# Six of sixteen images: the last two slots' statistics taken one slot at a time, with the instruction streams merged anew

## What is computed

```python
x = x + conv_block(group_norm(x, groups=32))
# conv_block: 1x1 convolution 768 -> 16, four "experts" of a 3x3 convolution at
# four resolutions, weighed by a gate (top 2 of 4), 1x1 convolution 16 -> 768
h = mean(xc over pixels) @ H_w.T + H_b        # xc: the 16-channel images
g = softmax(h where among the top two, else -inf)
out = sum(experts * reshape(g, (4, 16, 1, 1, 1)))
```

## Time and profile before

| | |
|---|---|
| median of 3 runs | 1462.71 us (1459.87 to 1462.95) |
| the profiled execution's own time | 1463.79 us |
| its span, first to last instruction | 1462.1 us |
| busy: PE 1206.2, DVE 1028.5, ACT 661.6, POOL 314.9 us | 82%, 70%, 45%, 22% of the span |
| moved by the DMA engines | 540.01 MB, mean 369 GB/s |
| mean granted TensorE clock | 0.88 of full speed |

### The profile page before, as it was taken

One profiled execution on the slowest core, in us unless ns is written; L12 is line 12 of the kernel. 1 busy time (PEld: TensorE's weight loads), 2 busy tenths in 40 slices (PEclk: granted clock), 3 DMA queues, 4 the chain that ended last, 5 costly groups with the idle time before them and its releaser, 6 DMA issues.

```text
span 1462.1 us, 24056 instructions
## 1 busy us (share of the span) xinstructions
PE 1206.2 (82%) x8700; PEld 818.7 (56%) x8700; DVE 1028.5 (70%) x2747; ACT 661.6 (45%) x1549; POOL 314.9 (22%) x381
## 2 busy tenths in 40 slices
...
DMA  9798996699999999999999999999999999999998
GB/s 343 263 363 301 344 345 260 241 368 343 410 391 394 404 356 368 378 386 385 376 396 386 380 378 346 382 359 391 378 379 382 405 413 411 408 411 413 396 383 356
DMA packets 188162, 540.01 MB, mean 369 GB/s; under 512 B 12810, under 2 KB 12810, under 8 KB 188044
## 3 DMA queue, kind: packets, MB, share of 16 engines
...
## 4 chain that ended last, share of the span: by engine, by line
PE 43%; DMA 28%; DVE 13%; ACT 6%; SPq 5%; issue 4%; POOL 1%; DVEq 0%; ACTq 0%; POOLq 0%
PE ring_ps L680 15%; DMA x_sb<-in_x 14%; DMA out<-x_sb 14%; PE conv_ps L750 10%; DVE x_sb L1004 9%; PE ring_ps L781 8%; PE img_ps L697 8%; SPq L512 3%; ACT xT L803 3%; DVE stats L920 2%; SPq L483 1%; PE ring_ps L769 1%; ACT unread_copy L827 1%; ACT unread_squares L825 1%; PE ring_ps L710 1%
## 5 line engine op out<-in xcount | busy, mean ns | idle before, releaser
L1004 DVE TENSOR_TENSOR x_sb<-x_sb,ring_ps 128x768 f32<-128x768 f32 x512 | 460.4, 948 | 312.0 <-PE ring_ps L781 186.3
L920 DVE BATCH_NORM_STATS2 stats<-x_sb 128x6 f32<-128x192 f32 x1792 | 473.0, 343 | 44.7 <-DMA x_sb<-in_x 39.4
L803 ACT COPY xT<-ring_ps 128x1024 f32<-128x1024 f32 x384 | 376.3, 1012 | 228.9 <-PE ring_ps L680 165.4
L680 PE MATMUL ring_ps<-ident,x_sb 128*128 128x128 f32 x3072 | 399.8, 283 | 66.8 <-DMA x_sb<-in_x 25.4
L680 PEld LDWEIGHTS ring_ps<-ident,x_sb 128*128 128x128 f32 x3072 | 348.7, 145 | 146.4 <-issue 89.4
L781 PE MATMUL ring_ps<-w,es 128*128 128x512 f32 (+1 forms) x1024 | 334.5, 443 | 111.7 <-DVE x_sb L1004 84.4
L781 PEld LDWEIGHTS ring_ps<-w,es 128*128 128x128 f32 x1024 | 188.5, 229 | 237.9 <-DVE x_sb L1004 148.6
L643 POOL TENSOR_TENSOR band<-taps,masks 128x640 f32<-128x640 f32 (+1 forms) x112 | 133.0, 1204 | 492.9 <-PE conv_ps L750 489.1
L750 PE MATMUL conv_ps<-xc,band 128*128 128x1 f32 (+8 forms) x1120 | 235.1, 360 | 4.0 <-issue 2.7
L697 PE MATMUL img_ps<-xT,w 128*32 128x256 f32 x3072 | 218.4, 393 | 16.9 <-ACT xT L803 13.2
L750 PEld LDWEIGHTS conv_ps<-xc,band 128*128 128x128 f32 x1120 | 168.0, 207 | 79.0 <-issue 76.2
...
## 6 DMA issues: line engine op xcount, KB each, us to landing
x_sb<-in_x SPq DMA_DIRECT2D x128, 1536.0 KB, 11.4
out<-x_sb SPq DMA_DIRECT2D x256, 768.0 KB, 10.4
...
wl_raw<-in_L_conv_convl_w SPq DMA_DIRECT2D x8, 9.0 KB
gate_w<-in_L_conv_H_w SPq DMA_DIRECT2D x8, 0.2 KB
...
b_raw<-in_L_conv_conv_b SPq DMA_DIRECT2D x2, 3.0 KB
```

The costliest lines, as they stand in the source:

```text
L680: last = nc.tensor.transpose(ring_ps[:, buf, q, half * P:(half + 1) * P], slot("L", a, 2 * c + half)[:, q, k * P:(k + 1) * P], ident[:, :])
L803: nc.scalar.copy(xT[:, at % XT], ring_ps[:, TURN["T", a, n] % RING]).then_inc(xT_copied, 1)
L920: ins = nc.vector.bn_stats(stats[:, c, g, :], group)
L1004: nc.vector.tensor_tensor(x_sb[:, n, 2 * half + q % 2, :], x_sb[:, n, 2 * half + q % 2, :], flat_ps[:, TURN["E", b, t] % RING, 0:D], ALU.a ...
```

## The change

`SINGLE` was 0 and becomes 6: for the first six images of order A the last pair of slots (6 and 7) is no longer one part of the statistics but two, each of one slot. Their moments have five parts where there were four. An instruction over one slot has 96 elements per partition where one over two slots has 192. The instruction gives the same kind of moments for its halves, of half as many elements, so the means are halved first (a new DVE instruction on 128 x 56) and then squared. All four lists are merged anew; the pieces in them are the same but for the new ones (`B12.4`, `S12.4` and so on, the fifth parts). The number of transfers and their bytes are unchanged, and so are the places and `KEPT`.

```diff
-SINGLE = 0
+SINGLE = 6
...
 PE_ORDER
-... T12.17-18 ... T12.20-22 M12.18 T12.23 M12.19-20 Z0 M12.21 T0.0 ...
+... T12.17 ... T12.21-22 M12.20 T12.23 T0.0 Z0 M12.21 T0.1 ...
 ACT_ORDER
-S0.1.30-31 T12.7-12 S0.2.28-29 T12.13-15 S0.2.30-31 T12.16 S0.3.28 T12.17-19 S0.3.29 T12.20 S0.3.30-31 T12.21-23 S4.0.28 D0
+S0.1.30-31 T12.6-8 S0.2.28-30 T12.9 S0.2.31 T12.10-14 S0.3.28-29 T12.15 S0.3.30 T12.16-18 S0.3.31 T12.19 S0.4.28-29 T12.20 S0.4.30-31 T12.21-23 T0.0 D0
```

More of the change, by code:

```diff
@@ new lines @@
+S8.7.0 R14.3.1:7.1 S8.7.1 R14.4.0:0.0 S14.0.0 S14.0.1 S14.1.0 S14.1.1 S14.2.0 R14.4.1:0.1 R14.5.0:5.0 S14.2.1
+R14.5.1:5.1 R14.6.0:6.0 S14.3.0 S14.3.1 S14.4.0 S14.4.1 R14.6.1:6.1 R14.7.0:7.0 R14.7.1:1.0 R13.0.0:1.1 R13.0.1:7.1
+S14.5.0 S14.5.1 S14.6.0 R13.1.0:0.0 S14.6.1 S14.7.0 R13.1.1:0.1 R13.2.0:5.0 R13.2.1:5.1 R13.3.0:6.0 S14.7.1
+R13.3.1:6.1 S13.0.0 S13.0.1 S13.1.0 S13.1.1 S13.2.0 R13.4.0:7.0 R13.4.1:7.1 R13.5.0:1.0 R13.5.1:1.1 S13.2.1
+R13.6.0:0.0 R13.6.1:0.1 R13.7.0:5.0 R13.7.1:5.1 S13.3.0 S13.3.1 S13.4.0 S13.4.1 S13.5.0 S13.5.1 S13.6.0 S13.6.1
@@ L96 @@
+S13.7.0 S13.7.1 S15.0.0 S15.0.1 S15.1.0 S15.1.1 S15.2.0 S15.2.1 S15.3.0 R12.0.0:10.0 R12.0.1:6.0 R12.1.0:6.1 S15.3.1
+S15.4.0 S15.4.1 S15.5.0 S15.5.1 S15.6.0 R12.1.1:10.1 S15.6.1 S15.7.0 R12.2.0:9.0 R12.2.1:9.1 S15.7.1 S12.0.0
+R12.3.0:8.0 S12.0.1 R12.3.1:8.1 R12.4.0:10.0 S12.1.0 S12.1.1 S12.2.0 S12.2.1 R12.4.1:6.0 R12.5.0:7.0 R12.5.1:7.1
+S12.3.0 R12.6.0:6.1 R12.6.1:10.1 S12.3.1 S12.4.0 S12.4.1 R12.7.0:8.0 R12.7.1:8.1 S12.5.0 S12.5.1 S12.6.0 S12.6.1
+S12.7.0 S12.7.1
 """
 PE_ORDER = """
-V T12.0-3 Z12 T12.4 M12.0-4 T12.5-8 M12.5 T12.9-10 M12.6-8 T12.11-12 M12.9-10 T12.13 M12.11-12 T12.14-17 M12.13-14
@@ L143 @@
-M15.18-20 T15.21 X8.2 T15.22 E8.14 M15.21 T15.23 M15.22-23 E8.15 X8.3 G3 E8.16 H3 E8.17-30 C14.0-1 E8.31 C14.2-6
-X14.0-1 E14.0-9 C13.0 E14.10-13 C13.1 X14.2 E14.14-15 X14.3 E14.16-18 C13.2 E14.19 C13.3-6 E14.20-26 C15.0-5 E14.27-31
-X13.0-1 E13.0-13 C15.6 X13.2 E13.14-15 X13.3 E13.16-22 C12.0-1 E13.23 C12.2-4 E13.24-31 X15.0-1 E15.0-12 C12.5-6
-E15.13 X15.2 E15.14-15 X15.3 E15.16-31 X12.0-1 E12.0-13 X12.2 E12.14-15 X12.3 E12.16-31
+V T12.0-2 Z12 T12.3-5 M12.0-3 T12.6-8 M12.4-8 T12.9-12 M12.9-10 T12.13-14 M12.11 T12.15-16 M12.12 T12.17 M12.13-15
@@ new lines @@
+T12.18 M12.16-17 T12.19-20 M12.18-19 T12.21-22 M12.20 T12.23 T0.0 Z0 M12.21 T0.1 M12.22-23 T0.2 W T0.3 M0.0-1 T0.4
+M0.2 T0.5-7 M0.3-6 T0.8-9 M0.7-8 T0.10-12 M0.9-12 T0.13-17 M0.13-14 T0.18 M0.15 T0.19 M0.16 T0.20 M0.17 T0.21 M0.18-20
+T0.22 Z4 T0.23 M0.21 T4.0 M0.22 T4.1 M0.23 T4.2-3 M4.0 T4.4 M4.1 T4.5-6 M4.2-4 T4.7-9 M4.5-6 T4.10 M4.7 T4.11 M4.8
+T4.12 M4.9-10 T4.13-14 M4.11-12 T4.15-16 M4.13-14 T4.17 M4.15 T4.18 M4.16 T4.19 M4.17 T4.20 M4.18-19 T4.21-22 Z8 T4.23
+M4.20 T8.0 M4.21 T8.1 M4.22-23 T8.2 M8.0 T8.3 M8.1 T8.4-6 M8.2-3 T8.7 M8.4 T8.8 M8.5-6 T8.9 M8.7 T8.10 M8.8-9 T8.11
@@ L147 @@
+C12.4-6 E15.9-13 X15.2 E15.14-15 X15.3 E15.16-31 X12.0-1 E12.0-13 X12.2 E12.14-15 X12.3 E12.16-31
 """
 ACT_ORDER = """
[L152 to L155 removed]
@@ L171 @@
[L171 to L175 removed]
+S12.0.28-31 S12.1.28-31 S12.2.28-31 S12.3.28-30 T12.0 S12.3.31 S12.4.28-31 T12.1-2 D12 S0.0.28-31 S0.1.28 T12.3
```

229 lines of the change are left out of this document (111 added, 118 removed).

## The result

The changed kernel takes 1494.2 us (median of 4, 1485.6 to 1497.7), the kernel before in the same measurement 1462.8; the ratio is 1.0193, interval 1.015 to 1.0235. Timed again later beside experiments it took 1490.2 us (6 runs) for 1465.7: 1.0152, interval 1.012 to 1.0185. By the two ratios it is 22 to 28 us slower (by the medians 24 to 31). The direction was forecast; the size, 13 us with 1486 as the upper end, was about half.

What follows compares the result with a forecast made beforehand. DVE and ACT bound the early images, transfers the rest. 6.4 at image 0 plus four times 2.8 less 0.6 is 17.0; less 4.0 given back, 13.0 us: 1476 us, with 8 in 10 at 1462 to 1486.

Steps and rivals of the forecast that it cites:

- What bounds it: Early, DVE and ACT have nearly no room; late, transfers never stop, so a delay ahead of them moves the end.
- The price of slot by slot: First six images: finer statistics cost DVE 2.8 us an image (0.9 to 8.0) and ACT 2.0 us.
- Image 0: Four ACT copies move behind the load wait and groups take longer: fold +6.4 us, near 104.3, image 12's 2.8 included.
- Images 4, 8 and 3: DVE goes on back to back: each adds 2.8 us, less 0.6 once because image 4 no longer waits for W's transposition.
- Image 2: DVE back to back adds another 2.8 us; the fold ends at 277.7 for 260.8, 17.0 later in all.
- That last step: From Z2 to the first addition: 15.4 us for 19.4, as 6.85 us of convolution moves ahead of Z2; 4.0 given back.
- The late lists: New instruction lists after 300 us: not costed, taken as hidden under the transfers if they keep them fed.
- My own sign of being wrong: After 300 us: the forecast would be wrong if the transfer rate there, 381 GB/s, moved by more than 1%.
- the late transfers: Rival, 300 to 1200 us: better-mixed reads and writes give the delay back; faster, say 1457, chance 0.08; about all, 0.10.
- Price by elements: Rival on the statistics: 0.130 us a step, DVE 0.9 an image, ACT's 2.0 sets the pace; 1466 to 1469, chance 0.12.
- finer statistics: Rival at images 12 and 0: DVE starts sooner on single slots, at most 2.3 us each; 1459, chance 0.03.
- ACT and PE jam: Rival: Z4 ahead of T0.23 holds up loads; images 4 to 2 lose 2 us more each; 1484 to 1490, chance 0.13.

Runs made afterwards that it cites:

- four_copies_behind: Kernel before, with ACT's copies 9 to 12 of image 12 moved behind the first two groups of image 0's third pair: 1469.3 us, 1.0026.
- conv_ahead_of_sum: Kernel before, with PE's first three convolution pieces (6.85 us) put ahead of image 2's sum of moments: 1474.6 us, 1.0054.
- singles_only: Kernel before in its own lists, with the fifth parts of the first six images put right behind the fourth: 1479.5 us, 1.0106.
- merge_only: Changed kernel's lists without the fifth parts, all statistics in pairs (SINGLE = 0): 1486.0 us, 1.0154 to the kernel before.
- gates_first: Changed kernel, with PE's matmul spreading image 3's gates put ahead of two transpositions: 1488.0 us, 1.0148 to the kernel before.

## Why the prediction was half right

**What bounds it: right.** Each early delay that reached the first store came through to the end of the profiled execution: +3.8 gave +3.8 in `four_copies_behind`, +8.8 gave +8.7 in `conv_ahead_of_sum`, +14.1 gave +15.7 in `singles_only`. The medians agree (+3.4, +8.7, +14.5). DVE and ACT are both near full in the early images, as the earlier trace rows had it.

**The price of slot by slot: right.** 2.6 us an image for the 2.8 forecast on DVE, and a group of one slot takes ACT 0.67 us as forecast. `singles_only` alone cost +14.1 at the first store. The Trainium skill, "Perfetto Trace Analysis", section "Optimizing Scalar/DVE Operations", puts about 60 ns on each DVE instruction on SBUF. The trace agrees: 0.260 us a step at 192 elements and 0.160 at 96 are 1.04 ns an element and 60 ns beside.

**Image 0: right mechanism, undersized.** +6.4 forecast; +8.7 and +7.0 in the two executions. I had ACT's copies behind the load follow each other at 0.92 us. Between 78 and 98 us they wait 3.7 us in all for PE's projections and transpositions, so that ACT's groups ended at 98.4 and 96.9 where I had near 96, and the sum behind `T0.0` at 102.2 where I had 98.4 to 100.3. The shift by four copies alone, forecast at 4, measured 3.8.

**Images 4, 8 and 3: somewhat oversized.** +7.8 forecast with the 0.6, +5.4 measured (+1.4, +1.1, +2.9). In the old lists `singles_only` has just the 7.8 there; in the new ones a part lies beside PE's and ACT's work. At image 8 the fold ends 5.3 us after DVE's statistics for 6.5: the sum ends 1.6 after them for 2.2, and the fold itself takes 3.6 for 4.2. The errors at image 0 and here cancel: 228 at image 3 was right, by luck.

**Image 2: the step that failed early.** "DVE goes on back to back, so each adds its 2.8" gave image 2 one more 2.8; it took 8.0 (+14.1 to +22.1), in the second execution 6.9. And "6.85 us of the convolution stand ahead of Z2, under statistics that DVE is still taking" had the wrong overlap: the convolution ended at 277.3, 5.9 us after DVE's statistics. I had read the new lists at image 0 and at the first addition, and not between image 3's fold and `Z2`. There, 9 of ACT's 20 groups of image 2 stand behind image 3's `xc` (none did before), where they end 5.1 us after DVE's statistics. It is the order that does this and not the 2.0 us that the fifth parts add on ACT: `merge_only`, without them, loses 6.4 us at image 2, while `singles_only`, with them in the old lists, loses 2.6 and has ACT just under DVE. DVE, too, is 3.4 us later by the gates, whose spreading now stands behind two transpositions; `gates_first` shows that this is not in the sum.

In the forecast's own terms: `Z2` was to end 17.0 us later than before (254.64) and ended 24.4 later, at 279.06. From there to the first addition are 16.2 us for 19.4, so 3.3 were given back where I had 4.0. That last step was costed nearly right, and without the move the first store comes 7 us later.

**The late lists: the step that failed late.** "Not costed: the new instruction lists after 300 us" is worth about 6 us. I had seen the sign, more reloads four halves behind their store (110 to 128) and said that this "rather slows than speeds", but put no number on it. I took a DMA share of 1.00 for a rate that stays; in the changed kernel's profile it moved between 373 and 394 GB/s at a share of 0.99 to 1.02. My own sign of being wrong, more than 1% on the rate after 300 us, would hardly have caught it: from 300 to 1200 us the two profiles have 379 and 376 GB/s for 381.

Together: +13.0 forecast at the first store, +21.1 and +18.4 measured, then the late 6 us: 24 to 27 together, where the ratios say 22 to 28. Of the rivals, the late transfers gave nothing back (they cost 6 us). *Price by elements* fails on the 2.6 us an image, and finer statistics let nothing start sooner: in `singles_only` the folds of images 12 and 0 end 2.3 and 3.7 us later. *ACT and PE jam* came nearest in size, 1484 to 1490, and has half the mechanism: ACT and PE do end last, but at image 2; images 4, 8 and 3 lose less than forecast and not 2 us more, and the convolution did give something back.

**What stays open.** Which property of the new late lists costs the 6 us. And the scatter: of the changed kernel's two profiled executions the second has its first store 2.8 us earlier and yet ends 5.4 us later, so that the stretch behind it differs by 8 us; nothing here shows why.
